# Multiplications of the identity with itself in three waits of TensorE, in a decoder layer with two attentions and a mixture of experts

## The reference

```python
x = x + self_attention(layernorm(x), weight_qkv, weight_proj)      # 16 heads of 128, 4 key/value heads, causal
x = x + cross_attention(layernorm(x), ctx, mask, Wq, Wk, Wv, Wo)    # 16 heads, 8 key/value heads, 64 context rows
x = x + experts(layernorm(x), gate, w0, w1, wo)                     # 8 experts of 512, the best two of each token

# experts, of a token with the two largest gate logits a >= b:
weights = softmax([a, b])
out = sum(weight_e * ((silu(x @ w0[e]) * (x @ w1[e])) @ wo[e]) for e in the two)
```

## Time and profile before

| | |
|---|---|
| time of the runs | 941.53 us median of 3 (941.32 to 941.83) |
| the profiled execution | span 942.9 us; of this execution no other time is on record |
| PE busy | 857.6 us (91%), 5165 multiplications |
| DVE, ACT, POOL busy | 547.9 us, 444.5 us, 270.5 us |
| chain that ended last | PE 75%, DVE 7%, DMA 7%, ACT 3% |
| longest waits of PE | 12.4 us for the first loaded rows, 9.6 us for the first normalised rows, 6.4 us for the last group's packed rows |

### The profile page before, as it was taken

How to read it: one execution, slowest core, us unless ns; L and a number is a source line. 1 busy time by engine, 2 the same in 40 slices (tenths; PEclk the granted TensorE clock), 3 DMA queues, 4 the chain that set the end, 5 groups by cost and what they waited for, 6 DMA issues and landing times.

```text
span 942.9 us, 15579 instructions
## 1 busy us (share of the span) xinstructions
PE 857.6 (91%) x5165; PEld 738.0 (78%) x5166; DVE 547.9 (58%) x1579; ACT 444.5 (47%) x1130; POOL 270.5 (29%) x397
## 2 busy tenths in 40 slices
PE   5899999999999999998888989989753999999995
PEld 4788889988899889997765868868652787888884
DVE  5677656665666656564666776858756622222221
ACT  3766665665656665665442443343433522222221
POOL 1233222323233223223011120513561323232322
PEclk9999999999999999999999999999976999999998
DMA  8000998000000000002063454437993233333332
GB/s 310 3 2 20 300 298 218 1 1 1 2 1 1 23 2 1 1 22 69 24 121 58 90 111 90 107 65 183 250 356 114 40 48 49 50 50 50 51 50 29
DMA packets 62913, 76.89 MB, mean 82 GB/s; under 512 B 3328, under 2 KB 54656, under 8 KB 62720
## 3 DMA queue, kind: packets, MB, share of 16 engines
q1 hardware_dynamic: 55104, 64.61, 26.8%
q0 software_dynamic: 7744, 11.44, 7.0%
HBM read 30.65 MB, written 28.61 MB: 63 GB/s over the span
## 4 chain that ended last, share of the span: by engine, by line
PE 75%; DVE 7%; DMA 7%; ACT 3%; issue 3%; SPq 2%; POOL 1%; another core or an unknown queue 0%; POOLq 0%; DVEq 0%; ACTq 0%
PE bank_y L1746 7%; PE bank_s L40 5%; PE bank_s L42 5%; PE bank_s L41 5%; PE bank_o L40 4%; PE bank_t L471 4%; PE bank_o L42 4%; PE bank_o L41 4%; PE bank_y L40 4%; PE bank_q L40 4%; PE bank_y L42 4%; PE bank_y L41 4%; PE bank_q L41 4%; PE bank_q L42 4%; DMA b_VW_lo<-b_VWs_lo 3%
## 5 line engine op out<-in xcount | busy, mean ns | idle before, releaser
L267 POOL TENSOR_TENSOR a_prob<-a_prob,a_rinv 128x128 f32<-128x128 f32 (+1 forms) x256 | 124.2, 506 | 310.2 <-DVE a_rinv L358 308.0
L329 DVE TENSOR_TENSOR a_pT_lo<-bank_t,a_pT_hi 128x384 fp32r<-128x384 f32 x128 | 70.5, 551 | 103.1 <-ACT a_pT_hi L281 103.1
L281 ACT ACTIVATE a_pT_hi<-bank_t 128x384 fp32r<-128x384 f32 x128 | 62.8, 491 | 120.1 <-PE bank_t L471 120.1
L292 ACT ACTIVATE a_prob<-a_masked,a_negmax 128x128 f32<-128x128 f32 (+1 forms) x256 | 113.9, 454 | 0.0
L1105 POOL DMA_INDIRECT out_dram<-b_y,b_rows x39 | 62.8, 1611 | 160.1 <-DVE b_y L1522 157.1
L1515 DVE TENSOR_TENSOR b_xT_lo<-bank_o,b_xT_hi 128x256 fp32r<-128x256 f32 x39 | 16.6, 425 | 119.4 <-ACT b_xT_hi L1224 119.4
L391 DVE CUSTOM_DVE_ANT_0 a_masked<-bank_s,a_causal 128x128 f32<-128x128 f32 (+1 forms) x256 | 80.2, 350 | 9.2 <-PE bank_s L42 9.2
L40 PE MATMUL bank_s<-a_kT_hi,a_qT_hi 128*128 128x128 f32 (+1 forms) x256 | 80.8, 315 | 0.0
L1746 PE MATMUL bank_y<-b_We,b_interT 128*128 x312 | 75.4, 384 | 2.0 <-issue 1.2
L40 PE MATMUL bank_y<-a_WprojT_hi,a_oT_hi 128*128 128x256 f32 x256 | 72.7, 284 | 0.5 <-DVE a_oT_lo L329 0.5
L42 PE MATMUL bank_y<-a_WprojT_hi,a_oT_lo 128*128 128x256 f32 x256 | 72.2, 282 | 0.0
(11 more groups left out here) (335 smaller groups left out, 2408.2 us busy)
## 6 DMA issues: line engine op xcount, KB each, us to landing
slots<-a_nobody SPq DMA_DIRECT2D x1, 16641.0 KB, 67.3
b_VW_hi<-b_VWs_hi SPq DMA_DIRECT2D x16, 512.0 KB, 6.2
b_VW_lo<-b_VWs_lo SPq DMA_DIRECT2D x16, 512.0 KB, 9.9
b_W<-in_L_ffn_w_kernel_dram SPq DMA_DIRECT2D x16, 512.0 KB, 6.2
b_rows<-slots SPq DMA_DIRECT2D x39, 129.0 KB
b_We<-in_L_ffn_wo_kernel_dram SPq DMA_DIRECT2D x8, 512.0 KB
a_stage<-n_L_attn_weight_qkv_dram SPq DMA_DIRECT2D x5, 512.0 KB, 8.6
x_WqT<-in_L_xattn_Wq_dram SPq DMA_DIRECT2D x1, 2048.0 KB, 8.4
```

Of the source, the lines that this page charges most:

```text
L267: pool.tensor_tensor(prob[:, u % 3, a:b], prob[:, u % 3, a:b], rinv[:, u % 4, i:i + 1].to_broadcast([P, b - a]), ALU.mult)\
L281: act.activation(dst.hi, src, ACT.Copy).then_inc(half[n], 1)
L292: act.activation(prob[:, u % 3, a:b], masked[:, u % 2, a:b], ACT.Exp, scale=-1.0, bias=negmax[:, u % 4, i:i + 1], accum_out=rowsum[:, u % ...
L329: dve.tensor_tensor(dst.lo, src, dst.hi.bitcast(F32), ALU.subtract).then_inc(free[n], 1)
```

## The change

A new helper issues a number of multiplications of a 128x128 matrix with itself on PE, each into the same 128 columns of a bank, each starting a new sum. It is called in three places with the identity: 20 times between PE's wait for the identity and its wait for the first normalised rows (into bank s0); 16 times in slot (PAIRS, 1), between the rank of the last group but one and the transposes of the last group's rows (into bank o1); and 36 times behind the last slot, ahead of the first expert tile (into o1). No semaphore is counted by them or waited for, and their results are overwritten unread.

```diff
+def keep_busy(pe, out, square, times):
+
+
+    for _ in range(times):
+        pe.matmul(out, square, square, start=True, stop=True, skip_group_check=True)
...
         pe.wait_ge(ident_made, 2)
+        keep_busy(pe, bank["s0"][:, 0:P], ident[:], 20)
         pe.wait_ge(xn_ready, TT)
         fill(first[0][0])
         fill(first[1][0])
...
                 if t < 3 and earlier_tile(p, t, 1):
                     transposes(*earlier_tile(p, t, 1))
+                if (p, t) == (PAIRS, 1):
+                    keep_busy(pe, bank[IT_BANK][:, 0:P], ident[:], 16)
                 for name in fills_at(p, t, 1):
                     fill(name)
                 if t == 3:
                     transposes(*earlier_tile(p, t, 1))
+            keep_busy(pe, bank[IT_BANK][:, 0:P], ident[:], 36)
```

## The result

The changed kernel takes 935.11 us (median of 20 runs, 931.09 to 942.41), the kernel before 940.90 (20 runs, 936.89 to 943.29). The ratio is 0.9944 with a 95% interval of 0.9928 to 0.9959: 5.3 us faster, 3.9 to 6.8. Three executions among the later runs, of 1097 to 4398 us, are left out of every median and ratio here. Gains in us are taken from the ratio, not from the difference of the medians.

What follows compares the result with a forecast made beforehand. PE was taken to bound the kernel (75% of the chain), its clock low after waits. Start -2.8, middle -0.5 and experts 0 gave -3.3 us: span 942.9 to 939.6, median 941.53 to 938.2 us, range 936.6 to 941.4.

Steps and rivals of the forecast that it cites:

- Start, -2.8: 20 calls before the first rows: transposes 0.6 us earlier, projections at full clock 2.2 us, together 2.8 us saved.
- Rival 1: Start's clock falls again before the first projection; only transposes gain, -0.6 there and -0.5 in the middle: 940.4 us, chance 37%.
- No later step hangs on a fixed moment, so I let the 2.8 pass to the end: After the start: the 2.8 us won there was taken to reach the kernel's end whole.
- Middle, -0.5: 16 calls before the last group's transposes: full clock for the transposes, 0.5 us saved; bounds +0.2 and -1.3.
- Experts, 0: 36 calls before the first expert tile: clock expected lost in the waits behind, nothing counted; bounds -1.4 and +2.6.
- Rival 2: All three places: the identity's zeros do not raise the clock, sum +3.1 to +3.3, 944.7 us; chance 9%.
- Rival 3: Start as forecast, plus experts' first tile at full clock (-1.4) or part of 3.3 us before 697.03: 936.8 or less; 9%.
- The range: Whole kernel: eight-in-ten range of 936.6 to 941.4 us, taking in the forecast and rival 1.
- theory A: Experiments at the start: streaming 128 columns counts; transposes raise the clock, 3 to 5 us gained; 8-column multiplications do not, within 0.6.

Runs made afterwards that it cites:

- seven unchanged profiles: Profiles whose program is that of the kernel before up to 687 us: its first, three repeats, and three kernels with only the middle or experts calls.
- again_2: The kernel before, unchanged, profiled again (third profile): 940.98 us.
- start_only: Kernel before plus only the 20 calls at the start: 936.32 us against 941.85, ratio 0.9950.
- start_plus: Kernel before plus the 20 start calls and 6 more between the eight transposes and the first projection: 935.76 us against 941.56, ratio 0.9935.
- start_covers: Kernel before plus the 20 start calls and 8 and 10 calls in two waits of cross-attention: 936.28 us against 942.79, ratio 0.9934.
- start_transposes: Kernel before plus 36 transposes of the identity at the start, in place of the 20 calls: 934.93 us against 941.56, ratio 0.9933.
- start_narrow: Kernel before plus 18 multiplications of the identity by its first 8 columns at the start, in place of the 20 calls: 938.46 us against 941.56, ratio 0.9962.
- again_1: The kernel before, unchanged, profiled again (second profile): 944.05 us.
- middle_two: Kernel before plus only 2 calls, not 16, before the last group's transposes: 940.91 us against 941.85, ratio 0.9999.
- one cover: Kernel before plus 8 calls in cross-attention's wait before 444 us: 939.39 us, ratio 0.9966; two: also 10 in the wait before 467, 936.65 us, 0.9942.

## Why the prediction was wrong

- *Start, -2.8:* right. The calls end before 9.5, their spacing halves on the way, the projections take 0.23, the first scores come 2.98 us earlier (forecast 18.0, seen 17.82). The spacing halved 5.3 us after the first call, later than the 3.2 to 4.8 taken, and the calls ended at 8.96, not 7.9 to 8.6; the wait hid that. Against the mean of the seven unchanged profiles the lead is 2.6, as the clock's first rise varies among them (17.9 us in before, 15.9 in again_2). Rival 1, clock lost again before the projections, did not happen in the profiles of after, start_only, start_plus and start_covers. It can happen: start_transposes' profile shows it, with a longer pause.
- *"No later step hangs on a fixed moment, so I let the 2.8 pass to the end":* the step that failed. The lead passes self-attention unchanged, but the steps of cross-attention did not just follow: three of its waits came out otherwise. From 437 to 687 the mean of the seven unchanged profiles moves by 0.2 against before's (-0.4 to -0.6), that of after, start_only and start_plus by 1.7 (-3.0 to -4.7). So some 1.5 us came on top of 2.6: 4.1 by 687.
  - Up to 476 they win 3.3 against a mean of 1.9, since the falls at 444 and 467, of some 1.6 us each, stay away in all three, and in four of the seven.
  - From there to 513 they win 1.2 where the others lose 0.2, most of it at the transfer's wait, which goes with the added calls and not with the lead.
  - Up to 634 they lose 3.2 against 1.6, mostly at the low clock and the longer wait from 608 on; start_narrow has that wait without the start's lead.

  In the times, start_plus's 3.6 to 8.7 leaves out 2.6 and 2.8; start_only's 2.4 to 7.0 takes both in, and so does not decide. The changed kernel's own time does not either: 2.6 with the 1.3 and 0.55 of the next two points is some 4.5, inside 3.9 to 6.8. Only three profiles stand against seven, so the 1.5 is an estimate, and no experiment switched one of these waits alone with everything ahead of it unmoved.
- *Middle, -0.5:* mis-sized in the trace. Both the transposes and the gate were at full clock, 0.5 + 0.8 = 1.3, the bound and not the value taken; the clock outlived 0.78 us of wait between them. Timed alone it is 0.4 us faster, with nothing excluded from 2.4 faster to 1.7 slower.
- *Experts, 0:* right in kind. 711.27 came after a wait of 2.22, and from 713.51 on the intervals were slow. Three fast intervals (0.33 + 0.23 + 0.24 against three sevenths of 3.15) gave 0.55 us; timed alone 1.5 us, not told from nothing.
- *Rival 2, the identity's zeros:* refuted, the 40 records sped up. It had no part in the time.
- *Rival 3, "part of the 3.3 us before 697.03":* its time came true (936.8 or less) by luck. The wait was chance in one profile; leaving it out of the sum was right.
- *The range:* it carried the unknowns of the three places, and nothing for the scatter of later waits, which from 437 to 687 spans 2.9 us among the unchanged profiles (again_1 loses 1.7, middle_two gains 1.2). It also stood on few runs: 941.53 was the median of three, and twenty gave 940.90, 0.6 of the 3.1 us between 938.2 and 935.11. The profile that was costed was of an execution at the slow end: in after's profile a span of 932.3 goes with a time of 934.03, so that the 942.9 stand for some 944.6, an estimate, above all twenty.

Open stays why start_narrow gained 3.6 us: the transfer's wait gives about 1 of it, and its start is known from its slowest run alone. Open also stays why one cover gained 3.2 and two 5.5, where a fall costs 1.6 and was seen in three of seven profiles; the transfer's wait gives 1.1 and 1.2 of these. That the position of later waits decides over the clock is consistent with all of it. It is shown for the waits at 444, 467 and 608 that their falls differ; that the position is the cause is argued.

## What to carry to other kernels

A wait of PE like those of 2.2 to 4.2 us here can have a second price, the clock for what follows; idle multiplications that end just before the data arrive take it away where the work behind them is long (eleven projections), and bring little where another wait follows. Before costing a change from one profile, take several of the unchanged kernel: falls of the clock and single odd waits that differ between them are scatter and not terms of a sum. A profile's own time belongs beside those of the other runs: here the two profiles that were hardest to read, start_transposes' and start_narrow's, were among the slowest runs of their kernels. A lead of a few us won early is kept through a dense stage, but can grow or shrink at every wait behind it, so its value is measured at the end and attributed stage by stage. Added work can also change waits far behind it that are not the clock's, as those for the transfer at 500 us and for the routing at 608 here.

## What the runs showed of the chip

- Transposes of the identity raised the granted clock: 36 in 5.46 us, and eight real ones behind them at 0.66 and 0.60. 36 records of plain f32 multiplications of 8 columns, in 7.85 us, were followed by work at the low clock. Each is one execution, and each is what theory A of its expectation said.
- The same wait of 2.18 us in the same program kept the clock in one run and lost it in another. The Trainium skill (TensorE: Matmul & The Clock Gate, Part 1, "What's actually happening") says that the monitor runs on its own and does not begin anew with a kernel, so that the moment of a change varies. The traces agree in that the moment varies: of the kernel before, the mark at 22 us varies by 0.9 us between four profiles, and the falls later on differ.
- A wait for the routing's rows grew where work had been added far ahead of it: before the fill at 608 us PE waited 4.20 us in the changed kernel, 4.19 in start_narrow, and 2.33 to 2.54 in seven profiles of the program before. What in the added work does it is not shown.
- Work added on one engine went with a shorter wait of another for a transfer: with eight or more extra calls ahead, ACT's wait near 500 us was 1.94 to 2.36 us in ten kernels, without them 2.83 to 3.21 in eight profiles.
